# Context rows normalised in turned form, from a second copy of the context with its axes exchanged

## The reference, cut to what matters

```python
# x: (4, 128, 512); context: (4, 2048, 512); 16 heads of 64; everything fp32
lat = layer_norm(_layernorm(x));  ctx = layer_norm(context)     # over the last axis, with gain g and offset b
q = lat @ Wq;  k, v = split(ctx @ Wkv)
k = apply_rope(k, cos, sin)
attn = softmax(clip(q @ k.T * 64 ** -0.5, -11, 11))             # 128 queries against 2048 context rows
x = x + (attn @ v) @ Wo + bo
x = x + linear_attention(_layernorm(x))                         # 16 heads of 32, key-value products
x = x + mixture_of_experts(_layernorm(x))                       # 8 experts, 2 of them for each row, and a shared one
```

## Time and profile before

| | |
|---|---|
| median of 3 runs | 1433.24 us (1431.34 to 1437.60) |
| profiled execution, device time | 1435.82 us |
| its span, first to last instruction | 1434.1 us |
| TensorE busy | 1383.0 us, 96% of the span |
| VectorE, ScalarE, GpSimd busy | 853.2, 796.5, 829.8 us |
| granted TensorE clock, mean | 0.990 of full |

### The profile page before, as it was taken

One profiled execution on the slowest core, in us unless ns is written; L12 is line 12 of the kernel. 1 busy time (PEld: TensorE's weight loads), 2 busy tenths in 40 slices (PEclk: granted clock), 3 DMA queues, 4 the chain that ended last, 5 costly groups with the idle time before them and its releaser, 6 DMA issues. The chain is left out here.

```text
span 1434.1 us, 25248 instructions
## 1 busy us (share of the span) xinstructions
PE 1383.0 (96%) x8758; PEld 1131.0 (79%) x8758; DVE 853.2 (59%) x1422; ACT 796.5 (56%) x1237; POOL 829.8 (58%) x721
## 2 busy tenths in 40 slices
PE   5899999999999999999999999999999999999998
PEld 3578888888788888888888888888888666766654
DVE  6356566566565656665565566665556556657554
ACT  3356666666565666665566666666645512446552
POOL 3267767777676777776677776777766343200002
PEclk9999999999999999999999999999999999899999
DMA  6567676667566666756666766766687545469994
GB/s 240 185 114 131 117 133 107 123 121 133 107 124 123 119 125 115 136 113 122 123 119 111 129 118 130 139 110 117 101 187 133 142 147 183 167 236 360 356 354 141
DMA packets 115267, 218.44 MB, mean 152 GB/s; under 512 B 13360, under 2 KB 49200, under 8 KB 108976
## 3 DMA queue, kind: packets, MB, share of 16 engines
q1 hardware_dynamic: 111968, 209.00, 64.9%
q0 software_dynamic: 1280, 4.20, 0.9%
q10 hardware_dynamic: 1872, 3.41, 0.6%
HBM read 132.67 MB, written 16.78 MB: 104 GB/s over the span
## 5 line engine op out<-in xcount | busy, mean ns | idle before, releaser
L610 POOL TENSOR_TENSOR p_parts<-probs,p_parts 128x512 fp32r<-128x512 f32 x256 | 341.3, 1352 | 249.5 <-ACT p_parts L668 249.5
L668 ACT ACTIVATE p_parts<-probs 128x512 fp32r<-128x512 f32 x256 | 147.7, 625 | 239.0 <-PE banks L978 231.1
L794 DVE TENSOR_TENSOR probs<-banks,probs 128x1024 f32<-128x1024 f32 x128 | 156.7, 1224 | 147.6 <-ACT probs L674 147.6
L698 ACT ACTIVATE probs<-probs 128x1024 f32<-128x1024 f32 x128 | 135.8, 1061 | 144.4 <-POOL probs L617 144.4
L930 PE MATMUL banks<-wv_hi,x_hi 128*128 128x512 f32 x512 | 208.5, 407 | 4.8 <-PEq L170 4.8
L931 PE MATMUL banks<-wv_lo,x_hi 128*128 128x512 f32 x512 | 203.0, 396 | 0.0
L945 PE MATMUL banks<-x_hi,wk_hi 128*128 128x512 f32 x512 | 201.8, 394 | 0.0
L932 PE MATMUL banks<-wv_hi,x_lo 128*128 128x512 f32 x512 | 201.7, 394 | 0.0
L947 PE MATMUL banks<-x_hi,wk_lo 128*128 128x512 f32 x512 | 199.6, 390 | 0.0
L946 PE MATMUL banks<-x_lo,wk_hi 128*128 128x512 f32 x512 | 199.3, 389 | 0.0
L974 PE MATMUL banks<-p_parts,v_hi 128*65 128x128 f32 x1024 | 191.7, 224 | 0.0
(11 more groups left out here) (296 smaller groups left out, 2682.4 us busy)
## 6 DMA issues: line engine op xcount, KB each, us to landing
queries<-q_scratch SPq DMA_DIRECT2D x256, 128.0 KB, 6.0
keys<-wo_room SPq DMA_DIRECT2D x128, 256.0 KB, 5.6
keys<-turned_odd SPq DMA_DIRECT2D x128, 256.0 KB, 5.6
row_room<-in_ctx SPq DMA_DIRECT2D x64, 256.0 KB, 6.2
wo_room<-in_down SPq DMA_DIRECT2D x10, 1024.0 KB, 8.0
late_room<-in_gate SPq DMA_DIRECT2D x8, 1024.0 KB
gate_raw<-in_up SPq DMA_DIRECT2D x8, 1024.0 KB, 9.8
up_raw<-in_gate SPq DMA_DIRECT2D x7, 1024.0 KB, 9.1
```

The lines of the kernel that those rows point to most:

```text
L610: nc.gpsimd.tensor_tensor(p_parts[:, 1, j, :], probs[:, pair % 2, j, :], p_parts[:, 0, j, :].bitcast(F32), ALU.subtract).then_inc(p_lo_rea ...
L794: nc.vector.tensor_tensor(mine, ps_s[:, :, :, 0, :].rearrange("p j i n -> p (j i) n"), mine, ALU.add).then_inc(s_taken, 1)
```

## The change

The host program passes the context a second time, as `ctx_t` with shape (64 tiles, 128 partitions, 4 blocks, 128 rows): each row tile with its columns on the partitions. Both copies are loaded: the one with rows on the partitions (`rows_early`, `row_in`) for mean and variance alone, the turned one into `xt`, where it is normalised in place. In turned form mean and factor differ along the free axis and are the same on all partitions. They are therefore stored to DRAM (`row_stats`, 128 rows of 8 bytes for a tile), loaded back broadcast to all partitions (`load_spread`, 1 KB for each partition), copied by ScalarE into the unused half of the PSUM bank of the sums (`ps_spread`), and used there by VectorE in two tensor_tensor operations over 128x512 (`centre_rows`); gain and offset follow on ScalarE in place, later in the step than before. In `prepare` VectorE does all of it, with the spread numbers in SBUF, and `prepare` takes the statistics of tiles 0 to 6. The transposes on TensorE go, in both parts. SyncE gets two waits more in odd iterations (for the factor, and for the landing of the stored statistics) and waits in even iterations for VectorE's measuring of a tile before it loads the next one.

```diff
-def load_row_tile(nc, r, sp, tile, slot):
...
-def normalise_row_tile(nc, r, dve, tile, slot):
...
-def transpose_row_tile(nc, r, pe, tile, slot):
...
-def scale_row_tile(nc, r, dve, tile, slot):
...
+def load_turned(nc, r, d, sp, tile, slot, landed):
+    sp.dma_start(r["xt"][:, slot], d["ctx_t"][tile]).then_inc(landed, 16)
+
+def load_spread(sp, to, stats, landed):
+    whose = stats.rearrange("r w -> (r w)").unsqueeze(0).to_broadcast([P, stats.shape[0] * 2])
+    sp.dma_start(to.rearrange("p n w -> p (n w)"), whose).then_inc(landed, 16)
...
 # prepare, SyncE
-            for i in range(ROW_TILES):
-                load_row_tile(nc, rows, sp, i, i)
+            sp.dma_start(rows_early[:, 0:ROW_TILES], rows["source"][0:ROW_TILES]...).then_inc(rows["pair_landed"][0], 16)
...
+            def store_stats(first, last, n):
+                sp.wait_ge(rows["rstd_ready"], n + 1)
+                sp.dma_start(d["row_stats"][first:last]..., row_mv[:, first:last]).then_inc(rows["stat_stored"], 16)
+                sp.wait_ge(rows["stat_stored"], 16 * (n + 1))
             load_piece(0)
+            sp.dma_start(rows["xt"], d["ctx_t"][0:ROW_TILES]...).then_inc(rows["spread_landed"], 16)
+            store_stats(0, ROW_TILES, 0)
+            load_spread(sp, spread_early..., d["row_stats"][0:ROW_TILES]..., rows["spread_landed"])
             load_piece(1)
             for m in range(PAIRS):
...
+                if m == 5:
+                    store_stats(ROW_TILES, MEASURED, 1)
+                    load_spread(sp, rows["spread"]..., d["row_stats"][ROW_TILES:EARLY]..., rows["spread_landed"])
+                    for tile in range(ROW_TILES, EARLY):
+                        sp.wait_ge(rows["lo_ready"], tile - ROW_TILES + 1)
+                        load_turned(nc, rows, d, sp, tile, tile % ROW_TILES, rows["pair_landed"][tile % 2])
...
+            for i in range(2):
+                sp.wait_ge(rows["pair_landed"][i], PAIR_BASE[i])
+            sp.wait_ge(rows["spread_landed"], SPREAD_BASE)
 # prepare, VectorE: in the loop over m, for m < ROW_TILES
-                    scale_row_tile(nc, rows, dve, m, m)
+                    centre_rows(m)
+            def centre_rows(tile):
+                if tile == 0:
+                    dve.wait_ge(rows["spread_landed"], 32)
+                mine = rows["xt"][:, tile]
+                for w, op in ((0, ALU.subtract), (1, ALU.mult)):
+                    link(nc.vector.tensor_tensor(mine, mine, spread_early[:, tile, :, w].unsqueeze(1).to_broadcast([P, KT, P]), op))
+                for k in range(KT):
+                    out = nc.vector.tensor_scalar(mine[:, k, :], mine[:, k, :], keep["ctx_g"][:, k:k + 1], keep["ctx_b"][:, k:k + 1],
+                                                  ALU.mult, ALU.add)
+                out.then_inc(rows["full_ready"], 1)
...
+                if m == 1:
+                    dve.wait_ge(rows["pair_landed"][1], 32)
+                    for i in range(ROW_TILES, MEASURED):
+                        stat = nc.vector.bn_stats(row_stats[:, i, :], rows_early[:, i, :])
+                    link(stat)
+                    rows_variance(ROW_TILES, MEASURED)
 # attend, SyncE, step(b, t)
-                    tile = row_tile_of(b, t + 5)
+                    tile = row_tile_of(b, t + 3)
                     if tile is not None:
-                        wait(sp, rows["tr_ready"], b * ROWS_OF_BATCH + (tile - 3))
-                        sp.dma_start(rows["row_in"][:, slot, :], rows["source"][b * ROWS_OF_BATCH + tile])...
+                        whole = b * ROWS_OF_BATCH + tile
+                        wait_alone(sp, rows["lo_ready"], whole - 3)
+                        load_turned(nc, rows, d, sp, whole, tile % ROW_TILES, rows["pair_landed"][tile % 2])
+                        if row_tile_of(b, t + 7) is not None:
+                            wait_alone(sp, rows["stats_ready"], whole + 1 - MEASURED)
+                            sp.dma_start(rows["row_in"][:, tile % 2, :], rows["source"][whole + 2])...
                     for pair in (t - 3, t - 2):
                         if exists(b, pair) and exists(b, t - 2):
                             load_queries(b, pair)
+                tile = row_tile_of(b, t + 2) if t >= 1 else None
+                if tile is not None:
+                    whole = b * ROWS_OF_BATCH + tile
+                    if not isinstance(whole, int) or whole >= MEASURED:
+                        wait_alone(sp, rows["rstd_ready"], STATS + whole + 1 - MEASURED)
+                        sp.dma_start(d["row_stats"][whole], rows["mean_var"][:, tile % ROW_TILES, :]).then_inc(rows["stat_stored"], 16)
+                        wait_alone(sp, rows["stat_stored"], 16 * (STATS + whole + 1 - MEASURED))
+                        wait_alone(sp, rows["spread_landed"], SPREAD_BASE + 16 * (whole - EARLY))
+                    wait_alone(sp, rows["spread_ready"], whole - 1 - ROW_TILES)
+                    load_spread(sp, rows["spread"][:, tile % 2], d["row_stats"][whole], rows["spread_landed"])
 # attend, ScalarE, step(b, t), after copy_scores
+                    wait(act, rows["spread_landed"], SPREAD_BASE + 16 * (b * ROWS_OF_BATCH + (tile + 1 - EARLY)))
+                    nc.scalar.activation(ps_spread, rows["spread"][:, tile % 2].rearrange("p n w -> p w n"),
+                                         ACT.Copy).then_inc(rows["spread_ready"], 1)
 # attend, VectorE, step(b, t)
-                    normalise_row_tile(...)            # stood ahead of take_scores
                 take_scores(b, t - SCORE_LAG)
+                    centre_rows(b, tile)               # behind take_scores
+            def centre_rows(b, tile):
...
+                mean, factor = (ps_spread[:, w, :].unsqueeze(1).to_broadcast([P, KT, P]) for w in range(2))
+                nc.vector.tensor_tensor(mine, mine, mean, ALU.subtract).then_inc(rows["xt_ready"], 1)
+                wait(dve, rows["xt_ready"], 2 * (whole - ROW_TILES) + 1)
+                nc.vector.tensor_tensor(mine, mine, factor, ALU.mult).then_inc(rows["xt_ready"], 1)
 # attend, TensorE
-                    transpose_row_tile(nc, rows, pe, b * ROWS_OF_BATCH + tile, tile % ROW_TILES)
 # weigh(b, pair)
-                        wait(pe, rows["full_ready"], b * ROWS_OF_BATCH + tile + 1)
+                        wait(pe, rows["xt_ready"], 2 * (b * ROWS_OF_BATCH + (tile - ROW_TILES + 1)))
 # host
+        "ctx_t": a["ctx_1024"].reshape(BATCH * CTX // P, P, KT, P).transpose(0, 3, 2, 1),
```

More of the change, by code:

```diff
@@ L37 @@
 VALUE_LAG = 5
+MEASURED = 7
+EARLY = 6
+STATS = 2
+PAIR_BASE = (32, 48)
+SPREAD_BASE = 48
 LHEADS = 16
@@ L130, in transpose_row_tile, with landings @@
-def transpose_row_tile(nc, r, pe, tile, slot):
[L131 to L135, removed]
-def scale_row_tile(nc, r, dve, tile, slot):
[L139 to L144, removed]
+def landings(b, tile):
+    last = isinstance(b, int) and b * (CTX // P) + tile + 2 >= BATCH * (CTX // P)
+    return PAIR_BASE[tile % 2] + b * (16 * CTX // P) + 32 * ((tile - EARLY) // 2) + (16 if last else 32)
@@ L275, in _, with rows_power @@
             latent_power(1, rstd_again[:])
-            for i in range(ROW_TILES):
-                row_tile_power(nc, rows, pool, i, i)
+            def rows_power(first, last, n):
+                pool.wait_ge(rows["var_ready"], n + 1)
+                nc.gpsimd.tensor_tensor(row_mv[:, first:last, 1], row_var[:, first:last], keep["minus_half"][:, first:last],
+                                        ALU.pow).then_inc(rows["rstd_ready"], 1)
+            rows_power(0, ROW_TILES, 0)
             weights_low(0)
@@ L333, in weights_low, with rows_variance @@
                                         ALU.subtract).then_inc(raw_lo[1], 1)
+            def rows_variance(first, last):
+                for i in range(first, last):
+                    stat = nc.vector.bn_aggr(row_mv[:, i, :], row_stats[:, i, :])
+                link(stat)
+                nc.vector.tensor_scalar(row_var[:, first:last], row_mv[:, first:last, 1], EPS, None, ALU.add).then_inc(rows["var_ready"], 1)
+            def centre_rows(tile):
[8 more added lines that the diff above has]
+                out.then_inc(rows["full_ready"], 1)
             for b in range(BATCH):
@@ L356, in _ @@
                                         scale[:, b:b + 1], ALU.subtract, ALU.mult).then_inc(norm_ready, 1)
-            for i in range(ROW_TILES):
-                dve.wait_ge(rows["stats_ready"], i + 1)
-                row_tile_variance(nc, rows, dve, i, i)
+            rows_variance(0, ROW_TILES)
             dve.wait_ge(small_landed, 16 * 4)
@@ L366, in _ @@
                 out.then_inc(lat_ready, 1)
-            for i in range(ROW_TILES):
-                normalise_row_tile(nc, rows, dve, i, i)
             weights_low(1)
@@ L438, in attend @@
         attn_t, wo = keep["attn_t"], keep["wo"]
[L439 removed]
+        bo = keep["bo"]
         banks = keep["banks"]
@@ L535, in early_loads @@
                 if t == BSTEPS - STEPS:
```

(14 more changed lines are left out.)

131 lines of the change are left out of this document (68 added, 63 removed).

## The result

The changed kernel takes 1495.21 us in the median of 4 runs (1485.76 to 1506.83), beside 1432.29 for the kernel before, measured along with it: 1.044 times the time, 95% interval 1.0391 to 1.049.

What follows compares the result with a forecast made beforehand. TensorE, 96% busy, was taken as the bound, each transpose group costing it 0.48 us. 1435.8 less 29.8 in `attend` plus 3.6 in `prepare` makes 1409.6, given as 1409 us; range 1403 to 1424.

Steps and rivals of the forecast that it cites:

- SyncE's loop: SyncE's odd iteration in `attend`: store, landing wait, then loads; 2.4 to 2.8 us to spare, no cost.
- SyncE's time to issue the loads, 4.3 us: After the landing in `attend`: spread load, two tile loads, four query loads and gaps take 4.3 us, until 265.9.
- on a queue that is now empty: First queries in `attend`, issued near 263, land 3.7 us later, by 267.4; their scores start at 269.8.
- The landing of 6.4: Statistics store behind the key moves in `attend` lands after 6.4 us; bounds 2.7 and something over 6.4.
- The third rival: SyncE's loop in `attend` becomes the bound if 8-byte rows land far later than 6.4; 1487 at 11.5; chance 0.07.
- The transposes: In `attend`, each transpose group costs TensorE 0.48 us; removing them with opening waits gains 29.8 us, in `prepare` nothing.
- The fourth rival: Transposes were not worth their time to TensorE, something else setting steps of 7.92 and 8.40: 1439 us; chance 0.03.
- VectorE fits: Odd step of `attend`: two added operations at 0.68 us each fit with 0.1 us to spare, no cost.
- The second rival: VectorE becomes the bound of `attend`'s odd step: 1437 us, half of it 1420; chances 0.06 all, 0.08 part.
- 3.6 (bound 10): `prepare`'s block ends near 58.4, 3.6 us later; bounds 0 if all is absorbed, about 10 if nothing is.
- The first round trip: In `prepare`, statistics through DRAM ahead of weight piece 1: VectorE's low part starts at 26.8, not 20.71, 6.1 us later.
- My bound of 10: Upper bound for `prepare`, 3.6 + 6.1, about 10 us, if nothing is absorbed; as a rival 1416 us, chance 0.14.

Runs made afterwards that it cites:

- the cheap load: Changed kernel with the spread load reading 128 different 1 KB pieces of the context instead of one piece 128 times: 1453.76 us, 1.014.
- the store-ahead kernel: Changed kernel with statistics stored ahead of the key moves in the even iteration, the wait kept in the odd one: 1419.26 us, 0.9884.
- the other runs: Three other runs with the changed kernel's `prepare` as it was; `attend` starts at 69.82 to 70.71 us.
- The mended kernel: Changed kernel with statistics stored before the key moves, `prepare`'s DMAs reordered and its last landing waits moved into `attend`: 1412.03 us, 0.9835.
- the kernel before with both DMAs: Kernel before plus statistics store, wait for its landing and spread load, data unused: 1482.61 us with one common piece, 1446.04 with 128 different pieces.

## Why the prediction was wrong, by its own steps

**The step that failed: SyncE's loop, "has 2.4 to 2.8 us to spare, and costs nothing on the path".** It named the right place and the right wait, and mis-sized the terms. It counted SyncE's time to issue the loads, 4.3 us, and not the time of the queue that carries them: the DMA engines are busy for 12.8 us of a turn that has no wait, and for 14.5 of a late one. The spread load stood in the sum as 0.6 us of issue; it lands 4.0 after its issue. And the queries went "on a queue that is now empty": it was empty of key moves, but the spread load and two tiles of 256 KB stood ahead of them, and they took 4.3 us in the median where the earlier trace rows gave 2.9 to 3.7.

The landing of 6.4, taken from the earlier trace rows, was right for the one undisturbed turn that it was worked out for, as if each turn began on time:

```profile
122.45 5.29 SPq L617 DMA_DIRECT2D keys<-wo_room  x4
127.78 0.59 SPq L596 DMA_DIRECT2D row_stats<-mean_var  x1
134.23 0.33 SPq L120 DMA_DIRECT2D spread_rows<-row_stats  x1
```

In a closed loop what is late goes round. The store at 127.78 lands in 6.4 us, the next three, at 143.9, 160.98 and 177.77, in 7.5, 8.6 and 10.0, while the four key moves ahead of each go out in 5.29, 4.12, 2.67 and 2.77 us; two loads of angles come in between, at 156.68 and 157.31. Over the run the store took 7.5 in the median of 57 and up to 11.5. The third rival described this and gave 1487, near the result, but by a landing of 11.5, which is the longest of the 57, and it held that nothing is lost up to 10.1. The median never came there and the loop failed all the same, so that the number was close is luck. The spread load's time is the one missing term that a run sizes (41 us); with the cheap load 34 us over the store-ahead kernel remain.

**The transposes were worth what was forecast.** Steps without a wait last 7.9, odd and even, and in the kernel with the store ahead all steady ones do (8.1 to 8.3 where finished sums are turned). The fourth rival falls.

**VectorE fits.** Its timeline in an odd step of the changed kernel (busy, then idle time in brackets):

```profile
130.48 0.68 DVE L891 TENSOR_TENSOR row_room<-row_room,banks 128x512 f32<-128x512 f32 x1
131.20 0.69 DVE L893 TENSOR_TENSOR row_room<-row_room,banks 128x512 f32<-128x512 f32 x1
...
133.34 0.15 DVE L906 TENSOR_SCALAR var_eps<-mean_var 128x1 f32<-128x1 f32 x1
133.63 0.69 DVE L806 TENSOR_TENSOR turned_odd<-banks,wo_room 128x512 f32<-128x512 f32 x1
```

0.68 and 0.69 for the two, and within 0.675 to 0.690 in all 60 tiles; 0.68 was taken from L803 of the earlier trace rows. The rotation (L806) starts 0.14 us after the end of the measuring (L906), with no late step. The second rival falls.

**`prepare`: 16.5 us later, for 3.6 (bound 10).** The first round trip did what was said of it, only later: VectorE's low part of piece 1 starts at 30.80 (20.71 in the earlier trace rows, 26.8 forecast): the store landed in 4.6 and not 2.7, and piece 1 stood behind a spread load that took 4.6 as well. Then VectorE beside GpSimd:

```profile
35.62 2.36 DVE L349 TENSOR_TENSOR row_room<-row_room,spread_early 128x512 f32<-128x512 f32 x2
38.02 3.04 DVE L351 TENSOR_SCALAR row_room<-row_room,ctx_g,ctx_b 128x128 f32<-128x128 f32 x4
```

The pair and the four small operations of the tile before took 1.41 and 1.12, near the 2.7 forecast for both; beside a GpSimd subtraction they take 5.4. Last, the second round trip:

```profile
56.17 0.79 SPq L225 DMA_DIRECT2D row_stats<-e_mean_var  x1
61.45 0.33 SPq L120 DMA_DIRECT2D spread_rows<-row_stats  x1
...
62.78 8.29 SPq L249 DMA_DIRECT2D q_scratch<-q_stage  x3
```

The store lands 5.3 us after its issue, with three query stores behind it. The first of these lands 6.5 us after its issue, ScalarE waits 7.1 us for it to free its buffer, and only then comes the last, which ends the block. My bound of 10 took only the first round trip as lost in full. Of the 16.5 the orders of SyncE and the waits at the end of the block account for 10.1 (71.63 to 61.51, together; 8.3 from the earliest start of the other runs). The rest, 6.4, is what normalising in turned form costs here as it stands, and perhaps 1 us of it comes from the four row tiles in one DMA. The Trainium skill, GPSIMD Engine Reference, section 1 (Specifications), says that GpSimd's SBUF interfaces are shared with VectorE and contended by instructions with two SBUF inputs. The prediction used it to expect GpSimd to be slowed; the traces show the price on VectorE as well (4.53 for 1.43) for the pair in `prepare`, and none for the pair in `attend`, which has an operand in PSUM. The four small operations, with one input in SBUF, paid too (3.04 for 1.12).

**The account of `attend`, 47.2 us after the first turns.** Idle time of TensorE is 52 longer. The transposes are gone, 27. The granted clock adds about 14: summed over windows of 4 us, length times the share not granted is 5.1 us before and 18.8 after; the stretches at the lower of the two levels (1.2 for 2.4 GHz) each come behind a wait. In the kernel with the store ahead it is 1.7. That makes 39; the other 8 are busy time of TensorE at the same clock, whose modelled ends don't let me place them.

**What stays open.** With the landing wait gone but the store still behind the key moves, 17 us remain over the store-ahead kernel, some 10 of them waits for scores (16.3 for 6.3). There the spread load waits in a full queue (7.3 to land) and so do the queries (4.8); no run separates what of that is the order of the queue and what its load. That keys, burst and landing feed each other, and that the angle loads push the loop over, is read from the timeline; no run held the burst fixed and varied the landing, or left the angle loads out.

**The whole.** The mended kernel, with the same computation, gives 1412 for the 1409 forecast. Its `attend`, from the first matmul to the last scores, is 30.2 us shorter than before (29.8 forecast), its `prepare` 6.4 longer (3.6 forecast): transposes and VectorE hold once SyncE has what the prediction said it had.

## What to carry to other kernels

An engine that issues all DMAs and waits in between for one of them to land closes a loop: add up for one turn the time that the DMA engines are busy with what the queue carries (DMA share times length of the window; not SyncE's time of issue, and not the landing times, which overlap) and the time in which the queue stands empty until the landing is known and the next transfers start, and compare that with the turn. Leave some room, since a late turn costs more than one that is on time. Where data goes out to memory and comes back, issue the store before the large transfers and put its wait behind them; that alone turned 1.044 into 0.988 here. A tensor moved to another form brings its own transfers, and those are to be costed on the queue like any other work.

## What the runs showed of the hardware

- One 1 KB piece read by 128 partitions lands later than 128 different pieces of 1 KB: 4.0 us against 2.4 in the changed kernel, 4.6 against 3.0 in the kernel before with both DMAs. In full loops that was worth 41 and 37 us. The one piece had been stored just before and the others lay in an input, so that it is the common address is not shown.
- Stores of 1 KB in rows of 8 bytes landed in 7.5 us (median) behind four moves of 256 KB and in 3.8 ahead of them. The Trainium skill, DMA: Bandwidth & Descriptors (Specifications), says that transfers under 512 B are done as read-modify-write; here the same small rows took 3.8 or 7.5 by their place in the queue, and what their size costs stays open, since no run gives the same store with larger rows.
- VectorE's pair of 128x512 operations with both inputs in SBUF took 1.43 us with GpSimd idle and 4.53 beside two GpSimd subtractions; with one operand in PSUM, 0.68 and 0.69 each, in all 60 tiles.
- Landings in a closed loop drift: 6.4, 7.5, 8.6 and 10.0 us for the same store in four turns, as the key moves ahead of it were issued in 5.29, 4.12, 2.67 and 2.77 us.
